# A two-layer sequence kernel on one core: both passages between its stages reordered, with matmuls that nobody reads added

## What is computed

```python
# layer 0: graph attention over the first 20 tokens, two directions d
self_feat = concat(v, q) @ W_self.T + b_self
aff  = (q_h . k_h) / 4 + label_bias            # softmax over 20 neighbours
out += softmax(aff) @ kv @ Wout + bout
x    = v + relu(out)
# layer 1: attention and feed-forward, both behind a conditioned layer norm
x1   = ln(x) * (scale1 + 1) + shift1
q, k, v = split(x1 @ mat_qkv_w.T + qkv_bias)
q, k = l2norm(q) * sm, l2norm(k)               # per head, 16 heads of 16
o    = softmax(q @ k.T) @ v
x    = x + (o @ proj_w.T + proj_b) * gamma1
x2   = ln(x) * (scale2 + 1) + shift2
x    = x + (gelu(x2 @ fc1_w.T + fc1_b) @ fc2_w.T + fc2_b) * gamma2
```

## Time and profile before

| | |
|---|---|
| runs | 793.78, 1425.53, 794.09 us |
| median | 794.09 us |
| the profiled execution | 790.3 us |
| its span, first to last instruction | 788.5 us |
| busy: PE, weight loads, DVE, ACT, POOL | 93%, 66%, 63%, 56%, 41% |

### The profile page before, as it was taken

How to read it: one execution, slowest core, us unless ns; L and a number is a source line. 1 busy time by engine, 2 the same in 40 slices (tenths; PEclk the granted TensorE clock), 3 DMA queues, 4 the chain that set the end, 5 groups by cost and what they waited for, 6 DMA issues and landing times.

```text
span 788.5 us, 15010 instructions
## 1 busy us (share of the span) xinstructions
PE 730.5 (93%) x4708; PEld 520.3 (66%) x4708; DVE 498.6 (63%) x1047; ACT 443.6 (56%) x733; POOL 322.8 (41%) x550
## 2 busy tenths in 40 slices
PE   4798999999996689999999999998889999999997
PEld 2587788888874345555555555555557888888885
DVE  2158999989988657767676767666515544434432
ACT  0325555555553367767676767666656555556553
POOL 1024655656554245555555555554542212222200
PEclk9989999999999799999999999999989999999999
DMA  8831334423311766667666776666500000000001
GB/s 240 294 88 43 116 84 125 117 80 115 116 32 32 126 160 136 146 149 147 147 148 146 142 150 148 146 147 154 132 14 1 28 13 14 27 29 27 14 27 40
DMA packets 83096, 79.65 MB, mean 101 GB/s; under 512 B 22942, under 2 KB 71710, under 8 KB 83054
## 3 DMA queue, kind: packets, MB, share of 16 engines
q1 hardware_dynamic: 81726, 78.95, 40.9%
q10 hardware_dynamic: 1328, 0.16, 0.1%
HBM read 57.13 MB, written 21.66 MB: 100 GB/s over the span
## 4 chain that ended last, share of the span: by engine, by line
PE 57%; ACT 6%; DVE 2%; issue 2%; POOL 1%; ACTq 0%; DVEq 0%; POOLq 0%
PE ps L1677 11%; PE ps L1691 11%; PE ps L1498 7%; PE ps L1570 6%; PE ps L1556 6%; PE ps L1608 4%; ACT probsT L912 4%; PE ps L1508 3%; PE ps L1589 2%; PE ps L1524 1%; PE ps L1601 1%; ACT part_pairs L935 1%; PE ps L1706 1%; PE ps L1662 1%; PE ps L1490 1%
## 5 line engine op out<-in xcount | busy, mean ns | idle before, releaser
L912 ACT ACTIVATE probsT<-ps 128x1024 f32<-128x1024 f32 x128 | 130.5, 1020 | 24.7 <-PE ps L1556 24.6
L1313 DVE TENSOR_TENSOR hidden_low<-hidden,hidden_high 128x512 fp32r<-128x512 f32 x64 | 46.1, 721 | 114.7 <-ACT hidden_high L1006 66.9
L1003 ACT ACTIVATE hidden<-ps,b_fc 128x512 f32<-128x512 f32 x64 | 44.1, 689 | 73.5 <-PE ps L1677 72.5
L1556 PEld LDWEIGHTS ps<-q_stack,k_stack 49*128 49x128 f32 x512 | 38.3, 185 | 60.3 <-ACT probsT L912 36.0
L1570 PE MATMUL ps<-probsT,v_ones 128*32 128x256 f32 x1024 | 70.2, 394 | 4.7 <-ACT probsT L912 4.5
L699 POOL TENSOR_TENSOR scores<-scores,row_max 128x640 f32<-128x640 f32 x32 | 42.2, 1318 | 76.7 <-DVE row_max L1042 76.7
L1556 PE MATMUL ps<-q_stack,k_stack 49*128 49x256 f32 x512 | 64.8, 331 | 7.9 <-ACT probsT L912 6.8
L1205 DVE TENSOR_REDUCE neg_max<-ps 128x4 bf16<-128x344 f32 x128 | 59.4, 506 | 15.2 <-PE ps L1524 15.2
L1498 PE MATMUL ps<-w_qkv,x1T 128*128 128x512 f32 x128 | 64.7, 628 | 3.2 <-DVE part_pairs L1212 3.2
L1416 PE MATMUL ps<-x_res,w_q 128*128 (+1 forms) x256 | 65.2, 400 | 0.0
L1416 PEld LDWEIGHTS ps<-x_res,w_q 128*128 128x128 f32 x256 | 48.5, 199 | 11.5 <-issue 5.5
(11 more groups left out here) (181 smaller groups left out, 1707.6 us busy)
## 6 DMA issues: line engine op xcount, KB each, us to landing
parts_dram<-part_pairs SPq DMA_DIRECT2D x64, 256.0 KB
q_stack<-parts_dram SPq DMA_DIRECT2D x96, 128.0 KB, 5.1
k_stack<-parts_dram SPq DMA_DIRECT2D x96, 128.0 KB, 5.6
adj<-in_adj SPq DMA_DIRECT2D x16, 440.0 KB, 3.4
xT<-in_xT SPq DMA_DIRECT2D x16, 256.0 KB, 2.7
x_res<-in_x SPq DMA_DIRECT2D x16, 256.0 KB, 3.4
x_in<-in_x SPq DMA_DIRECT2D x16, 256.0 KB, 2.7
gate_rows<-rows_dram SPq DMA_DIRECT2D x16, 256.0 KB, 7.0
```

Of the source, the lines that this page charges most:

```text
L912: nc.scalar.activation(probsT[:, s % 4, :], ps[:, COLS:COLS + 2, :].rearrange("p a n -> p (a n)"), ACT.Exp).then_inc(exp_made, 1)
L1003: nc.scalar.activation(hidden[:, s % RAW, :], ps[:, FC1[s % FC1_BANKS], :], ACT.Gelu, bias=b_fc1[:, m:m + 1]).then_inc(gelu_made, 1)
L1313: nc.vector.tensor_tensor(hidden_parts[1][:, s % H_SLOTS, :], hidden[:, s % RAW, :], hidden_parts[0][:, s % H_SLOTS, :], ALU.subtract).the ...
L1556: mm = nc.tensor.matmul(ps[:, COLS + j, kt * N:(kt + 1) * N], k_stack[at, par, s, kt * P:(kt + 1) * P], q_stack[at, par, s, :], start=True ...
```

## The change

Front passage. `FRONT = 2`: queries and keys of batch 1, too, are now made in the tail of the graph layer and no longer in turn 1, into the banks `FRONT_BANKS = (4, 5)`, and so are their `take_qk`, `square` and `sum_squares`, and `make_v` of batch 0. The roots of batch 1 go from DVE to POOL (`ROOTS_ON_VECTOR` 2 to 1). The writes of ones into `k_stack` go from SP's queue to ACT's. POOL's `blocks_of_pairs(0, 0)` waits no longer for `x_made`. `warm` is new: it multiplies the identity by a part of `w_qkv` into a bank that is free then; nobody reads the result. It stands three times between the row scores of turn 1 (512 columns each), and four times ahead of the first `col_scores` (512 columns each).

End passage. In turn 14 `make_v` goes from slot 2 to slot 0, the normalisation for the feed-forward layer from slots 4 and 8 to 0 and 4, `ffn_norm(0)` from the head of turn 15 to slot 7 of turn 14, `ffn_scale(0)` to its slots 8 and 9. In turn 15 `project` goes from slot 3 to slot 6 and `first` from slots 4 and 6 to 2 and 5. Five `warm` products are added: 384 columns in slots 1 and 2 and 256 in slot 6 of turn 14, 384 in slot 0 and 256 in slot 2 of turn 15.

The core of the diff; the rest of it follows from the words above.

```diff
-    FIRST_AT = (4, 6)
+    FIRST_AT = (2, 5)
-    ROOTS_ON_VECTOR = 2
+    ROOTS_ON_VECTOR = 1
...
+    FRONT = 2
+    FRONT_BANKS = (4, 5)
+
+    def in_turn(f):
+        return f is not None and not (isinstance(f, int) and f < FRONT)
+
+    def qk_bank(f, tt):
+        return FRONT_BANKS[tt] if isinstance(f, int) and f == 1 else QK_BANK + tt
+
...
+    def project_at(c):
+        return 6 if isinstance(c, int) and c == B - 1 else 5
+
+    def values_made_at(b):
+
+        return 0 if isinstance(b, int) and b == B - 1 else 2
...
-        for c in range(C2):
-            at = HALF * c + KROWS
-            sp.dma_start(k_stack[at:at + 1].bitcast(F32).rearrange("o a h n -> o (a h n)").rearrange("o (p e) -> o p e", p=P),
-                         ones_r[:]).then_inc(key_ones_in, 16)
...
             ahead = following(f)
             if isinstance(c, int) and c == B - 2:
+                ffn_root(0)
                 pool.wait_ge(g["late_weights"], g["LATE"])
                 split(w_fc1, w1_high, w1_low, w1_split)
...
         normalise(B - 1, 1, 1)
+
+        pool.wait_ge(q_mm, 2 * B)
+        blocks_of_pairs(0, 0)
         pool.wait_ge(x_made, B)
-        blocks_of_pairs(0, 0)
         nc.gpsimd.memset(v_ones[:, :, :, :, HD:2 * HD], 1.0).then_inc(ones_set, 1)
...
-                if b is not None and s == 3:
+                if b is not None and s == values_made_at(b) + 1:
                     take_v(b, 1 - par)
...
-                if isinstance(c, int) and c == B - 1 and s < C2:
-                    ffn_scale(0, (s,))
+                if isinstance(c, int) and c == B - 2 and s >= SLOTS - C2:
+                    act.wait_ge(s_mm, GROUPS * B)
+                    ffn_scale(0, (s - (SLOTS - C2),))
...
         take_weights(B - 2, 0)
+        square(0, 0)
         exponentials(B - 1, 1, 0)
         take_weights(B - 2, 1)
-        square(0, 0)
         exponentials(B - 1, 1, 1)
         square(0, 1)
+        shift_scale(1, 1)
         take_weights(B - 1, 0)
-        shift_scale(1, 1)
         take_weights(B - 1, 1)
         high(0, 0)
+        square(1, 0)
+        square(1, 1)
+        act.wait_ge(x_made, B)
+        for c in range(C2):
+            at = HALF * c + KROWS
+            act.dma_start(k_stack[at:at + 1].bitcast(F32).rearrange("o a h n -> o (a h n)").rearrange("o (p e) -> o p e", p=P),
+                          ones_r[:]).then_inc(key_ones_in, 16)
         turns(turn, act, 4, first=1, last=B + 2)
...
                 for n in groups(b, s):
                     maxima(b, n)
+                if isinstance(f, int) and f == 1 and s == 1:
+                    first_guess(f)
+                    for k in range(C2):
+                        nc.vector.tensor_scalar(b_gated[:, k, :], ada[:, k, :], b_proj[:, k:k + 1], None, ALU.mult).then_inc(gated_bias, 1)
                 if ahead is not None and s == 0:
                     norm_stats(nc, x_res, ahead, stats, stats_made)
                     dve.wait_ge(stats_made, T * (f + 2))
-                if f is not None and s == 1:
+                if in_turn(f) and s == 1:
                     sum_squares(f, 0)
...
-                if isinstance(f, int) and f < ROOTS_ON_VECTOR and s == 2:
-                    roots(f)
                 if d is not None and s == back_at(c):
                     divide(d)
-                if d is not None and s == back_at(c) + 3:
+                if d is not None and s == project_at(c) + 1:
...
                 if isinstance(c, int) and c == B - 2:
-                    if s == 4:
+                    if s == 0:
                         statistics(0)
                         ffn_moments(0)
-                    if s == 8:
+                    if s == 4:
                         dve.wait_ge(v_mm, B)
                         ffn_normalise(0)
...
-        take_qk(0, 0)
         sums(B - 1, 1, 0)
+        dve.wait_ge(g["late_weights"], g["LATE"])
         take_qk(0, 1)
         sum_squares(0, 0)
-        sums(B - 1, 1, 1)
         sum_squares(0, 1)
         first_guess(0)
+        sums(B - 1, 1, 1)
         take_output(B - 2)
         roots(0)
+        unit_qk(0)
+        take_qk(1, 0)
         graph_residual(B - 2, 0)
-        dve.wait_ge(g["late_weights"], g["LATE"])
-        unit_qk(0)
         take_output(B - 1)
+        take_qk(1, 1)
+        rests(0, 0)
         graph_residual(B - 1, 1)
+        sum_squares(1, 0)
+        sum_squares(1, 1)
         dve.wait_ge(x_made, B)
-        for k in range(C2):
-            nc.vector.tensor_scalar(b_gated[:, k, :], ada[:, k, :], b_proj[:, k:k + 1], None, ALU.mult).then_inc(gated_bias, 1)
-        rests(0, 0)
...
+        def warm(times, bank=None, columns=2 * F):
+
+            for j in range(times):
+                nc.tensor.matmul(ps[:, COLS + j % 2 if bank is None else bank, 0:columns], ident[:], w_qkv[:, 0, 0:columns], start=True, stop=True)
         def turn(f, b, c, d, par):
             for s in range(SLOTS):
-                if isinstance(c, int) and c == B - 1 and s == 0:
-
-                    ffn_norm(0)
+                if isinstance(c, int) and c == 0 and s == 0:
+                    pe.wait_ge(key_ones_in, 16 * C2)
+                    pe.wait_ge(wT_out, 2 * B)
+                    warm(4)
                 if c is not None and s < 8:
                     col_scores(c, par, s)
                 for n in groups(b, s):
                     row_scores(b, 1 - par, n)
-                if f is not None and s < 2:
+                    if isinstance(b, int) and b == 0 and n < GROUPS - 1:
+                        warm(1)
+                if isinstance(c, int) and c == B - 2 and s in (1, 2):
+                    pe.wait_ge(high_made, 2 * B)
+                    pe.wait_ge(rest_made, 2 * B)
+                    warm(1, QK_BANK, 3 * P)
+                if isinstance(c, int) and c == B - 1 and s == 0:
+                    warm(1, QK_BANK, 3 * P)
+                if in_turn(f) and s < 2:
                     make_qk(f, par, s)
-                if b is not None and s == 2:
+                if b is not None and s == values_made_at(b) and not (isinstance(b, int) and b == 0):
                     make_v(b, 1 - par)
...
                 if d is not None and s == back_at(c) + 1:
+                    if isinstance(c, int) and c == B - 1:
+                        pe.wait_ge(gated_made, d)
+                        warm(1, SIDE, F)
                     output_channels(d, f)
-                if d is not None and s == back_at(c) + 2:
+                if d is not None and s == project_at(c):
                     project(d)
                 if f is not None and s == 6:
...
+                if isinstance(c, int) and c == B - 2 and s == 6:
+                    warm(1, QK_BANK, F)
+                if isinstance(c, int) and c == B - 2 and s == 7:
+                    ffn_norm(0)
...
         norm_transposed(0, QK_BANK + 1)
         weights_of(B - 2, 0, 0)
-        raw_scores(B - 1, 1, 1)
         pe.wait_ge(g["late_weights"], g["LATE"])
         make_qk(0, 0, 0)
+        raw_scores(B - 1, 1, 1)
         weights_of(B - 2, 0, 1)
         make_qk(0, 0, 1)
+        pe.wait_ge(aff_out, 2 * T * B)
+        norm_transposed(1)
         graph_channels(B - 2, 0, B)
         weights_of(B - 1, 1, 0)
-        pe.wait_ge(aff_out, 2 * T * B)
-        norm_transposed(1)
+        make_qk(1, 1, 0)
+        weights_of(B - 1, 1, 1)
+        make_qk(1, 1, 1)
         graph_tokens(B - 2)
-        weights_of(B - 1, 1, 1)
         graph_channels(B - 1, 1, B)
         split_qk(0, None)
         graph_tokens(B - 1)
+        pe.wait_ge(qk_out, FRONT * T)
+        make_v(0, 0)
         turns(turn, pe, 4, first=1, last=B + 2)
```

25 lines of the change are left out of this document (12 added, 13 removed).

## The result

The changed kernel takes 787.69 us, the median of four runs (786.23, 787.51, 787.87, 788.08); the kernel before, timed beside it, 793.93 (one of its four runs, at 1425.53 us, is disturbed and left out of the ratio). The ratio is 0.9918, 95% interval 0.9900 to 0.9937: about 6 us, less than 2%. The prediction was 786.3 us in 782 to 792, so the total came out within 1.4 us. Where the time went did not come out as predicted either, and most of this text is about that.

The account below looks back on a forecast made before the run. PE idling in latency chains and losing its clock in two passages was taken as the bound. Profiled: 790.3 - 3.3 - 0.4 - 4.1 = 782.5 us; median: 794.1 - 7.8 = 786.3 us, range 782 to 792.

Parts of the forecast that it names:

- forecast 3.3 + 0.4 us: Front passage: first column scores at 269.05 instead of 272.34 (3.3 us), and a 0.36 us wait in turn 2 gone (0.4).
- the fetches as unmoved: Front passage: fetches into the stacks start at the same time as before; bounds 2.6 us earlier, 0.75 later.
- The maxima land 2.85 us after ACT has scaled them: Front passage, ahead of the first column scores: the row of maxima arrives at about 266.2, not late.
- The fetches fill the DMA engines until 268: Front passage: fetches into the stacks are through at about 268.4, before the column scores forecast at 269.05.
- rival 3: Front passage: stacks or maxima land as late as before, scores start at 272.3, no front gain; 789.6 us, chance 0.07.
- rival 1: Front passage: the clock is low all the same, costing 2.5 us; 788.8 us, chance 0.17.
- The four products: Products without a reader ahead of the first column scores: 3.9 us of work, 0.65 us of it on the path.
- The rule on GpSimd and VectorE: Front passage: shared SBUF interfaces could slow `normalise` of batch 2 beside POOL's roots by 0.95 us (787.0 us); priced 0.
- forecast 4.1 us: End passage, turn 15: clock 2.7, covered waits 1.1, projection 0.8, less product 0.5; bounds 1.4 and 5.5; turn 14 unchanged.
- the covered waits: Turn 15: waits of 0.93 and 0.21 us for `divide` and the bias are covered by first(0), gaining 1.1 us.
- Rival 2: End passage: the clock falls in turn 15 all the same, costing 2.7 us; 789.0 us, chance 0.13.
- Rival 4: Both passages: products without a reader run at half clock in PE's queue and don't lift it; 800.8 us, chance 0.05.

Follow-up runs that it names:

- e4: The changed kernel without its five products without a reader in turns 14 and 15; 789.44 us, ratio 0.9963 to the kernel before.
- e2: The end half of the change alone, on the kernel before; 787.56 us, ratio 0.9936 to the kernel before.
- e3: The changed kernel without its seven products without a reader in the front passage; 787.69 us, ratio 0.9929 to the kernel before.
- e8: The changed kernel without any of its twelve products without a reader, the order alone; 790.78 us, ratio 0.9990 to the kernel before.
- e1: The changed kernel with its end passage put back as before, the front half alone; 792.85 us, ratio 1.0012 to the kernel before.
- e12: The changed kernel itself, unedited, timed and profiled again; 787.91 us, ratio 0.9954 to the kernel before.
- e7: The changed kernel with batch 0's row of maxima issued from ACT's queue and six products instead of four ahead of the column scores; 788.18 us, ratio 0.9946.
- e5: The changed kernel with batch 0's row of maxima issued from ACT's queue instead of SP's; 788.41 us, ratio 0.9951 to the kernel before.

## Why the prediction was right in sum and wrong in its parts

**Front passage, forecast 3.3 + 0.4 us, found 0 (-0.04 between the marks; 2.4 in e4's execution).** The steps up to the transposes held or came early: `high` of batch 0 ended at 251.53 (I said 252.1), the first scores began at 254.57 (254.9), the roots on POOL ended at 262.01 (262.8), the transposes of batch 1 began at 263.33 (264.05). The first fetch went out at 257.25 where it went out at 257.27, so "the fetches as unmoved" held too. The step that failed is the one on what is late next: "The maxima land 2.85 us after ACT has scaled them; that would be at about 266.2", and "The fetches fill the DMA engines until 268 and then for 0.39 us more: about 268.4". The first took a time measured on idle engines to a place where they are full. The second took the fall of the share for the moment at which readers go on; the scores start 2.1 us after it in the changed kernel. By the table's formula the fetches of the kernel before, at the 154 GB/s of the earlier trace rows, release their reader at 257.27 + 10.2 + 3.0 = 270.5. Its scores began at 272.34, so in that execution the whole front passage could give no more than 1.9 us however early the maxima came; at 140 GB/s, 0.8; at e4's 158, 2.1, where e4's scores came 2.3 us earlier. The 3.3 us were never there. In e2, with the front as before and 137 GB/s, they'd be 274.38 - (259.32 + 11.5 + 3.0) = 0.6 us.

That was rival 3, to which I gave 7%. I held against it that the fetches "are through at 268.4", which is the failed step itself.

What was left of the gain, 1.0 us, went to the clock, as rival 1 has it but in another place: not between the row scores, where it held, but in the new wait of 3.63 us, which neither I nor the rival had. From the first column scores to those of turn 3 the kernel before took 20.22 us (272.34 to 292.56), the changed one 21.36 (271.49 to 292.85).

**The four products**, 0.65 us of my path, lay wholly in the wait; e3 without the seven runs as fast. **The rule on GpSimd and VectorE**: `normalise` of batch 2 took 0.90 us beside POOL's roots at 257.79 against 0.73, 0.2 us rather than the 0.95 that I had as upper bound, and with the front waiting for DMA it cost nothing. So the 0.95 us were not met, though the direction was right. Where DVE runs the four instructions of `ffn_normalise` beside the end of POOL's split of the weights and its residual sum, the contention is plain, and also hidden: 0.79 us each, against 0.34 for the same four in the kernel before, where POOL had nothing to do beside them (timeline of DVE, before, then changed kernel):

```profile
563.68 1.37 DVE L1301 TENSOR_SCALAR x_hat_f<-x_res,mean_var_f,rstd_f 128x256 f32<-128x256 f32 x4
```

```profile
559.28 3.17 DVE L1325 TENSOR_SCALAR x_hat_f<-x_res,mean_var_f,rstd_f 128x256 f32<-128x256 f32 x4
```

**End passage, forecast 4.1 us, found 3.90 in turn 15 and 0.53 in turn 14.** The terms held: the clock at 1.00, the waits for `divide` and the bias covered, first(0) without a queue behind it. e4 splits turn 15 along the terms of the sum: the order gave 2.0 us, where I had 1.1 for the covered waits and 0.8 for the projection, and the products 1.9, where I had 2.7 for the clock less 0.5 for the product on the path. The 0.53 us of turn 14 I had at nothing; they come from the order, since turn 14 takes 18.00 us in e4 and 17.96 in e8, without products. In e1, which has the old end, turn 14 took 20.04 us and turn 15 19.52: the same loss of clock, in 556 to 560 (0.58) instead of 572 to 576 (1.00). The place of the fall isn't fixed, so the end is better judged over both turns: 40.54 us before, 39.56 in e1, 38.03 in e4 and 36.11 in the changed kernel, whose repeat took the same (551.59 to 587.70).

Rival 2 (the clock falls in turn 15 all the same) was not the rule but does occur, in one of the ten profiles with the end products. In the profiled execution of e3, turn 15 began with a wait of 2.08 us for a fetch, and the products didn't hold the clock:

```profile
570.32 0.50 PE L1582 MATMUL ps<-q_stack,k_stack 49*128 49x256 f32 x4 [2.08 <-DMA k_stack<-parts_dram]
570.75 0.91 PE L1649 MATMUL ps<-w_qkv,ident 128*128 128x384 f32 x2
...
572.51 1.97 PE L1615 MATMUL ps<-ident,o_sumsT 128*128 128x128 f32 x8
```

It took 791.12 us, the slowest of that kernel's runs. Rival 4 (products at half clock on the path) didn't come: in the changed kernel the longest product is the 1.13 us for two rows at 254.82, where rival 4 has 1.86.

**The sum.** For the profiled execution I forecast 782.5 us and it took 786.2: the 3.7 us of the front are missing. The median came out only 1.4 us from the forecast because it lay 1.5 us above the profiled execution and not 3.8, as before. The base helped too: the forecast started from 794.1 us, while the medians of the kernel before in the later timings, of 11 to 23 runs each, were 791.4 to 792.2. From there my 7.8 us would have given 783.6 to 784.4, where the changed kernel took 787.91 in e12. So the median was met by luck, and the term that was mis-sized is the front's. Why the median lies nearer to the profiled execution than before, no run shows.

## What to carry to other kernels

When a wait on one chain is removed, work out when everything else that the reader waits for arrives, and from the same kind of moment: a DMA's time from issue to reader, read when the engines are idle (2.8 us here), says nothing of its time behind 1.5 MB (8.7 us). For a burst of fetches the volume over the rate in a window, plus a constant from a profile in which the reader did wait for it, gives the arrival to half a microsecond, but only once the rate of that execution is known: over 127 to 158 GB/s the answers lie 2.4 us apart, and a forecast needs that range. In this kernel products without a reader were worth their place where PE waits in small pieces within a turn and has work right behind (1.9 us), and not ahead of a long wait for data, which they only fill. And edits of two passages should be run one by one, since here the timed runs show a gain from one of them only.

## What was not expected of the hardware

The DMA engines moved 127 to 158 GB/s at the same busy share (1.15 to 1.18) with the same twelve fetches, from one execution to the next; with it the first column scores shift by 2.4 us (12.99 in e4 against 15.42 in e7 after the first fetch). After the share has fallen, the reader still waits about 2 us (2.1 in the changed kernel), with every engine idle in 270 to 271. And a row of maxima (two transfers of 8 KB) that goes through ACT's queue arrives no earlier than one in the queue of the fetches: e5 and e7 lie on the same line as the rest. Last, four DVE instructions that took 0.34 us each alone took 0.79 us beside POOL's work.
